# Weighing expert outputs on ScalarE, more plain scatters, and sums loaded lane by lane in a decoder layer's experts

## The reference

```python
scores = softmax(layernorm(x) @ classifier_weight.T)
_, topk_idx = top_k(scores + bias, 6)
w_full = zeros.at[token, topk_idx].add(2.5 * scores at topk_idx)
out0 = xn * w_full[:, 32:].sum(-1)                  # pass-through experts
for e in range(32):                                 # routed experts
    gate, up = split(xn @ Wgu[e].T, 2)
    out += w_full[:, e] * (silu(gate) * up @ Wd[e].T)
x = x + out
```

## Time and profile before

| what | value |
|---|---|
| median of three runs | 1355.96 us |
| the profiled execution's own time | 1358.42 us |
| its span, first to last instruction | 1356.6 us |
| mean granted TensorE clock | 0.975 |
| PE busy / DVE busy / ACT busy / POOL busy | 1219.4 / 736.0 / 872.1 / 742.6 us |
| first and last gate of the 128 tiles (L2337) | 1084.1 and 1312.2 us |
| last scatter begins (L2052) | 1326.4 us |

### The profile page before, as it was taken

One profiled execution on the slowest core, in us unless ns is written; L12 is line 12 of the kernel. 1 busy time (PEld: TensorE's weight loads), 2 busy tenths in 40 slices (PEclk: granted clock), 3 DMA queues, 4 the chain that ended last, 5 costly groups with the idle time before them and its releaser, 6 DMA issues.

```text
span 1356.6 us, 27882 instructions
## 1 busy us (share of the span) xinstructions
PE 1219.4 (90%) x8682; PEld 736.5 (54%) x8682; DVE 736.0 (54%) x2398; ACT 872.1 (64%) x1693; POOL 742.6 (55%) x814
## 2 busy tenths in 40 slices
PE   6999999999999886899999999999999799997862
PEld 4666776776676465433243324333232688986650
DVE  6666466557545648463136213623652666658863
ACT  5666456546546425678967996799989277765530
POOL 1776567557657503356026703652477577776771
PEclk9999999999999897999999999999999999999996
DMA  7976477668635521000011001010383766689988
GB/s 241 350 246 221 174 237 267 237 213 276 219 133 198 183 63 42 26 26 17 9 40 34 23 3 48 3 34 1 116 292 120 280 191 196 211 235 234 271 161 263
DMA packets 165940, 208.04 MB, mean 153 GB/s; under 512 B 13184, under 2 KB 147344, under 8 KB 165152
## 3 DMA queue, kind: packets, MB, share of 16 engines
q1 hardware_dynamic: 149664, 175.95, 39.7%
q0 software_dynamic: 16128, 30.26, 8.6%
HBM read 77.30 MB, written 128.86 MB: 152 GB/s over the span
## 4 chain that ended last, share of the span: by engine, by line
PE 56%; ACT 13%; DVE 10%; issue 9%; DMA 6%; POOL 3%; SPq 1%; ACTq 1%; DVEq 0%; POOLq 0%
PE sa_pf L354 11%; ACT xa_probs L1398 8%; PE xa_banks L1237 7%; PE xa_banks L1252 6%; PE sa_po L429 5%; PE sa_ps L403 5%; PE xa_banks L1120 5%; PE sa_ptr L414 5%; PE sa_pf L387 4%; PE mo_banks L2136 3%; DMA mo_xs<-rows 3%; DMA mo_w_all<-in_down_p 1%; PE mo_banks L2145 1%; PE mo_banks L2124 1%; ACT xa_q_aug L1344 1%
## 5 line engine op out<-in xcount | busy, mean ns | idle before, releaser
L1398 ACT ACTIVATE xa_probs<-xa_banks 128x1024 f32<-128x1024 f32 (+1 forms) x416 | 401.9, 1045 | 82.7 <-PE xa_banks L1237 81.8
L341 POOL TENSOR_SCALAR sa_probs<-sa_probs,sa_recip 128x128 f32<-128x128 f32 (+3 forms) x256 | 275.4, 1089 | 176.0 <-DVE sa_recip L592 175.8
L472 ACT ACTIVATE sa_probs<-sa_probs,sa_neg_max 128x128 f32<-128x128 f32 (+3 forms) x256 | 141.9, 555 | 148.2 <-DVE sa_neg_max L529 148.1
L1252 PE MATMUL xa_banks<-xa_probs,xa_v_one 128*17 128x512 f32 (+1 forms) x1664 | 218.7, 598 | 6.9 <-ACT xa_q_aug L1344 4.6
L1237 PE MATMUL xa_banks<-xa_q_aug,xa_k_aug 32*128 32x512 f32 (+1 forms) x1664 | 153.3, 442 | 13.4 <-issue 3.3
L2136 PE MATMUL mo_banks<-mo_xs_t,mo_gu 128*128 128x128 f32 x1024 | 138.0, 278 | 4.4 <-DVE mo_hidden_t L2337 4.4
L529 DVE CUSTOM_DVE_ANT_0 sa_probs<-sa_ps,sa_toeplitz 128x128 f32<-128x128 f32 (+3 forms) x256 | 115.5, 488 | 38.6 <-PE sa_ps L403 35.7
L2136 PEld LDWEIGHTS mo_banks<-mo_xs_t,mo_gu 128*128 128x128 f32 x1024 | 126.5, 194 | 6.6 <-ACT mo_xs_t L2186 3.5
L2193 ACT ACTIVATE mo_gu<-mo_w_all 128x512 f32 x128 | 80.7, 630 | 64.1 <-issue 49.8
L1237 PEld LDWEIGHTS xa_banks<-xa_q_aug,xa_k_aug 32*128 32x128 f32 (+1 forms) x1664 | 61.6, 179 | 106.4 <-ACT xa_probs L1398 75.7
L589 DVE COPY sa_pt<-sa_ptr 128x128 f32<-128x128 f32 (+3 forms) x128 | 62.8, 490 | 104.0 <-PE sa_ptr L414 103.9
(11 more groups left out here) (332 smaller groups left out, 2340.8 us busy)
## 6 DMA issues: line engine op xcount, KB each, us to landing
rows<-sa_blank SPq DMA_DIRECT2D x128, 548.0 KB, 3.6
mo_xs<-rows SPq DMA_DIRECT2D x128, 137.0 KB
slots<-sa_blank SPq DMA_DIRECT2D x48, 256.0 KB, 4.0
mo_slot_part<-slots SPq DMA_DIRECT2D x24, 512.0 KB, 6.1
parts<-sa_blank SPq DMA_DIRECT2D x51, 128.0 KB, 4.2
xa_raw<-in_ctx_t SPq DMA_DIRECT2D x24, 256.0 KB, 2.8
mo_w_all<-parts SPq DMA_DIRECT2D x24, 256.0 KB, 6.2
mo_w_all<-in_gate_up_p SPq DMA_DIRECT2D x2, 2816.0 KB
```

The source lines that it names most:

```text
L341: pool.tensor_scalar(probs[:, t % SLOTS, 0:w], probs[:, t % SLOTS, 0:w], recip[:, col:col + 1], None, ALU.mult).then_inc(probs_ready, 1)
L472: act.activation(probs[:, t % SLOTS, 0:w], probs[:, t % SLOTS, 0:w], ACT.Exp, bias=neg_max[:, i:i + 1], scale=-1.0, accum_out=sums[:, i:i ...
L1252: last = pe.matmul(banks[32 * i:32 * i + XD + 1, 6 + group % 2, :], v_one[b % 2][0:m, c, 4 * g + i, :], probs[0:m, (2 * j + i // 2) % RING ...
L1398: act.activation(probs[0:m, n % RING, :, :], banks[0:m, 2 * (n % 3):2 * (n % 3) + 2, :], ACT.Exp).then_inc(probs_ready, 1)
```

## The change

- `weigh` moves from DVE to ACT: in step t ACT weighs tile t-3, between `copy_rows` of t+2 and silu of t; the last three tiles follow the loop. It waits there also for `own_ready`.
- `PLAIN` goes from 72 to 80: 80 plain scatters, 48 with an add.
- The slot loads begin at tile 92 and come every 7/5 tiles, so they end at tile 124 instead of 125. Tokens are loaded at SP's tiles 48, 56 and 64.
- In the tail SP no longer waits for all lanes: when tile 125 has landed it loads its lane in four loads of 512 KB, after tile 126 that one's, and after tile 127 the last lane in eight loads of 256 KB, each of these behind the landing of one earlier load that has the same semaphore. DVE adds the first two lanes by batch (8 adds of 128x1024) and the last by chunk (8 adds of 128x512); PE's part is gone. SP stores eight chunks instead of four batches.

```diff
-PLAIN = 72
+PLAIN = 80
...
-    TOKENS_AT = {56: 0, 72: 1, 88: 2}
+    TOKENS_AT = {48: 0, 56: 1, 64: 2}
...
-    SLOT_LOAD_AT = [SLOTS_FROM + 9 * n // 5 for n in range(len(SLOT_LOADS))]
+    SLOT_LOAD_AT = [SLOTS_FROM + 7 * n // 5 for n in range(len(SLOT_LOADS))]
     SLOT_ADD_AT = [t - 2 for t in SLOT_LOAD_AT]
-    SUMS_PE = [1, 4]
-    SUM_ORDER = [0, 2, 1, 3, 5, 4, 6, 7]
+    LAST_TILES = range(N_TILES - LANES, N_TILES)
+    SLOT_LOADS_EACH = len(SLOT_LOADS) // SLOT_RING
...
         def part(c, lane, n=1):
-            at = (c * LANES + lane) * CHUNK * D
+            at = lane * TILES * D + c * CHUNK * D
...
+        def batch_landed(eng, n, b):
+            eng.wait_ge(parts_in[n * B + b], 16 * (1 + (SLOT_LOADS_EACH if n == 0 else 0)))
+
+        def chunk_landed(eng, c):
+            eng.wait_ge(parts_in[c], 16 * (2 + (SLOT_LOADS_EACH if c < B else 0)))
...
-            for i in range(SCATTERS):
-                sp.wait_ge(y_sent[i], 16 * (N_TILES // SCATTERS))
+            sp.wait_ge(gu_ready, N_TILES)
+            for n, t in enumerate(LAST_TILES):
+                lane = t % LANES
+                tile_landed(sp, t)
+                if n < LANES - 1:
+                    for b in range(B):
+                        sp.dma_start(part(2 * b, lane, 2), lane_rows(lane)[:, TT * b * D:TT * (b + 1) * D]
+                                     ).then_inc(parts_in[n * B + b], 16)
+                else:
+                    for c in range(TILES // CHUNK):
+                        batch_landed(sp, c // B, c % B)
+                        sp.dma_start(part(c, lane), lane_rows(lane)[:, c * CHUNK * D:(c + 1) * CHUNK * D]
+                                     ).then_inc(parts_in[c], 16)
...
+            def weigh(t):
+                act.wait_ge(y_psum, t + 1)
+                act.wait_ge(own_ready, t + 1)
+                if t >= Y_RING:
+                    tile_landed(act, t - Y_RING)
+                act.activation(y[t % Y_RING][:], banks[:, 4 + t % 2, 0:D], ACT.Copy, scale=own[:, t, 0:1]
+                               ).then_inc(y_ready, 1)
+
             for t in range(N_TILES):
                 if t + AHEAD < N_TILES:
                     copy_weights(t + AHEAD)
                     copy_rows(t + AHEAD)
+                if t >= 3:
+                    weigh(t - 3)
                 act.wait_ge(gu_psum, t + 1)
...
-                if t >= 2:
-                    weigh(t - 2)
...
+            for n, t in enumerate(LAST_TILES[:-1]):
+                for b in range(B):
+                    batch_landed(dve, n, b)
+                    last = dve.tensor_tensor(batch_tokens(b), batch_tokens(b), part(2 * b, t % LANES, 2), ALU.add)
+                chain.then_wait(last)
+            for c in range(TILES // CHUNK):
+                chunk_landed(dve, c)
+                dve.tensor_tensor(tokens(c), tokens(c), part(c, LAST_TILES[-1] % LANES), ALU.add
+                                  ).then_inc(out_ready, 1)
```

More of the change, by code:

```diff
@@ L1886, in experts @@
         out_ready = sem("out_ready")
-        sum_psum = sem("sum_psum")
         out_done = sem("out_done")
@@ L1896, in part, with batch_tokens @@
         def part(c, lane, n=1):
-            at = (c * LANES + lane) * CHUNK * D
+            at = lane * TILES * D + c * CHUNK * D
             return w_all[:, at:at + n * CHUNK * D]
+        def batch_tokens(b):
+            return (own_x[:] if b == LAST else acc[:, TT * b:TT * (b + 1), :]).rearrange("p t d -> p (t d)")
         def load_weights(sp, lo, hi):
@@ L1906, in first_weights @@
             load_weights(sp, FIRST_WEIGHTS // 2, FIRST_WEIGHTS)
-        def parts_landed(eng, c):
-            eng.wait_ge(parts_in[c], 16 * (LANES + len(SLOT_LOADS[c::SLOT_RING] if c < SLOT_RING else ())))
+        def batch_landed(eng, n, b):
+            eng.wait_ge(parts_in[n * B + b], 16 * (1 + (SLOT_LOADS_EACH if n == 0 else 0)))
+        def chunk_landed(eng, c):
+            eng.wait_ge(parts_in[c], 16 * (2 + (SLOT_LOADS_EACH if c < B else 0)))
         slot_rows = slots[SLOT_ROWS:, :].rearrange("(k p t) d -> p k (t d)", k=TOP_K, p=P)
@@ L1950, in run_sync @@
                 sp.dma_start(xs[:, t % X_RING, :], rows[bass.ds(at, P), :]).then_inc(xs_in[t % X_RING], 16)
-            for i in range(SCATTERS):
-                sp.wait_ge(y_sent[i], 16 * (N_TILES // SCATTERS))
-            for c in range(TILES // CHUNK):
[L1954 to L1962, removed]
+            sp.wait_ge(gu_ready, N_TILES)
[11 more added lines that the diff above has]
+                                     ).then_inc(parts_in[c], 16)
+            out_v = out.rearrange("b (t p) d -> p (b t) d", p=P)
+            for c in range(TILES // CHUNK):
+                sp.wait_ge(out_ready, c + 1)
+                sp.dma_start(out_v[:, CHUNK * c:CHUNK * (c + 1), :],
+                             tokens(c).rearrange("p (t d) -> p t d", d=D)).then_inc(out_done, 16)
+            sp.wait_ge(out_done, 16 * TILES // CHUNK)
         def more_consts(pool):
@@ L2160, in run_tensor @@
                     back(t - 2, chosen[t - 2])
[L2162 to L2169, removed]
         def run_scalar(act):
@@ L2208, in run_scalar @@
                 act.activation(silu[t % 2][:], banks[:, 2 + t % 2, 0:P], ACT.Silu).then_inc(silu_ready, 1)
+            for t in range(N_TILES - 3, N_TILES):
+                weigh(t)
         def run_vector(dve):
@@ L2338, in gate @@
                                   ).then_inc(h_ready, 1)
[L2340 to L2345, removed]
             def add_slots(n):
@@ L2364, in run_vector @@
                         add_slots(n)
-            weigh(N_TILES - 2)
-            weigh(N_TILES - 1)
             chain.then_wait(dve.tensor_reduce(zero_w[:], weights[:, :, E_ROUTED:], AX.X, ALU.add))
```

## The result

The kernel after takes 1350.1 us, the median of 13 runs (1344.97 to 1353.39), beside 1356.47 for the kernel before, measured with it. The measured ratio is 0.9946, interval 0.9934 to 0.9957; the two medians alone would give 0.9953. So it is 6 to 7 us faster. Measured again later (after_again), it came to 0.994 [0.9921, 0.996]. The forecast of 1344.3 was 0.9914 of the 1355.96 it started from: the sign and the range held, the gain is about 0.6 of what was forecast.

The account below looks back on a forecast made before the run. PE paces tiles to 80, DMA the slot-load stretch, POOL's scatters the end. Last scatter -8.0 and tail -3.7 make -11.7 us: 1358.42 profiled to 1346.7, median 2.46 lower, 1344.3 us; range 1334 to 1355.

Parts of the forecast that it names:

- Weighing on ACT, 0 before tile 80: First 80 tiles: weighing takes 0.46 us, holds ACT 0.36; 1.46 us a tile stays under PE's 1.575, so no cost.
- the 0.09 us for the operand: ACT's weighing: 0.09 us added to a plain copy's 0.369 for the per-partition scale, giving 0.46.
- rival 1: ACT becomes the bound before tile 80: 1.80 us a tile, 18 us more, 1362 us, slower; chance 0.13.
- Tokens earlier, tile 80 and tile 83: DVE's 6.29 us token wait goes; tile 80 scattered at 1216.9, tile 83 at 1222.5, some 8 us gained there.
- POOL, able to do 2.19 us a scatter, is right behind y: tile 115 at 1296: Slot-load stretch: DMA sets 2.30 us a tile, scatters keep up with y; 12 left at 1294.
- 0.9 us for later y's: ACT's weighing waits for row copies of tile t+3, so each y comes 0.9 us later, between nothing and 1.575.
- the last scatter 8.0 us earlier: End of the loop: the last adding scatter begins at 1318.4, 8.0 us earlier; bounds 2.5 and 21.6 us.
- The tail, -3.7: Tail: bytes set its length; first lane's loads start two scatters earlier, saving 3.7 us; bounds 0 and 6.
- Rival 2: POOL stays seven tiles behind, waiting for landings; it gains 2.5 us and the tail 2: 1351.5 us; chance 0.22.
- its two signs: Rival 2's signs: POOL waits for landings over 10 us, with more than 15 scatters left after the last slot load.
- Rival 3: DVE, not DMA, sets 2.06 us; freed of weighing, the loop runs ahead, POOL at 1.87: 1331 us; chance 0.10.

Follow-up runs that it names:

- a_dve: The kernel after with the weighing back on VectorE, two tiles back; ratio to before 0.992 [0.99, 0.9939].
- c_dve4: The kernel after with the weighing back on VectorE, two tiles back, and four lanes of adding scatters in place of three; ratio to before 0.9936.
- a_half: The kernel after with each slot load cut to one of its two choices, leaving half the slots' values out of the sums; ratio to before 0.9863.
- c_lanes4: The kernel after with four arrays for adding scatters instead of three, so a scatter waits for the tile four before it; ratio to before 0.9927.
- b_act: The kernel before with only the weighing moved to ScalarE, three tiles back; ratio to before 0.9984.
- the run that was to tell it: The kernel after with the weighing on VectorE, three tiles back instead of two; ratio to before 1.0038.

## Why the prediction was right in sign and too large

- **Weighing on ACT, 0 before tile 80: right, with more room than I took.** It takes 0.467 us (0.46 forecast; that is partly luck, since the exponential that gave the 0.09 us for the operand also accumulates a sum). ACT's shortest whole tile is 1088.54 to 1089.85, 1.31 us (1.46 forecast):

```profile
1088.54 0.63 ACT L2196 ACTIVATE mo_gu<-mo_w_all 128x512 f32 x1 [0.18 <-issue]
1089.07 0.36 ACT L2189 ACTIVATE mo_xs_t<-mo_banks 128x256 f32<-128x256 f32 x1
1089.34 0.47 ACT L2209 ACTIVATE mo_y<-mo_banks,mo_own 128x256 f32<-128x256 f32 x1
1089.69 0.28 ACT L2221 ACTIVATE mo_silu<-mo_banks 128x128 f32<-128x128 f32 x1
1089.85 0.64 ACT L2196 ACTIVATE mo_gu<-mo_w_all 128x512 f32 x1
```

  Issue stands ahead of the first weight copy and is missing ahead of the second, as in the earlier trace rows. So rival 1 did not come about. The first 80 gates took 0.8 and 3.0 us longer than before; but the two kernels like after with the weighing two tiles back on VectorE (a_dve, c_dve4) took 126.7 and 126.8 us, and those with it whole on ScalarE 125.0 to 128.6, so no share of ACT in it is shown. The rule of the Trainium skill that spoke for rival 1 ("ScalarE: Activation LUTs", Rules for kernel authors: multiply on VectorE) came out otherwise in the arrangement of before, where the move gained 2.2 us. In that of after it may be right (0.992 against 0.9946, not settled), but not by ACT's time. Its figure gave 0.49 us for the weighing; the trace has 0.467.
- **Tokens earlier, tile 80 and tile 83: right in the profiled execution.** Tile 80 went at 1216.3 (1216.9 forecast), tile 83 at 1222.0 (1222.5), the first slot load at 1219.5 (1220.5); after_again is 2.4 us later in all three.
- **"POOL, able to do 2.19 us a scatter, is right behind y: tile 115 at 1296": the step that failed.** The prices were right: 23 x 1.42 + 33 x 0.58 + 30 x 0.82 = 76.4 us of work in 70, 1.09, and the share was 1.08 (1.05 in after_again). But I divided them as if each tile's row load, scatter and slot loads went in step, so that gate and scatter would both come every 2.30 us. They don't: the gates, behind SP's row loads, came every 2.12 us and the scatters every 2.43, and POOL fell nine tiles behind instead of running right behind y. What sets a scatter's pace is the time to the landing of the one three before it, which grew from 6.95 to 7.28 us where POOL waited for it, and is 6.46 in a_half (five waits); a sum of DMA work does not hold that term. Nor was 1.05 full, as four lanes show (1.11). Half the slots' bytes (a_half) or one lane more (c_lanes4) each brought the last scatter 8 to 9 us nearer to gate 80 (10 against after_again), so the landings behind the slot loads are shown as the cause. The Trainium skill ("DMA: Bandwidth & Descriptors", SWDGE vs HWDGE vs iDMA) says that an engine takes turns between its internal queues, fed by SP's loads and by POOL's scatters; no run shows the turns themselves. The software queue's share is no fixed one: 35.9% in after, 41.1% with four lanes, 45.6% with half the slots' bytes.
- **0.9 us for later y's: about right.** From tile 60 to 79 the weighing starts 4.02 us after the gate, 3.39 before, so 0.6 more. From tile 87 to 119 it is 5.38 (before 4.38, a_dve 4.67), 1.0 us more; there it stands behind row copies that wait for the DMA, as shown under a_dve. I had named the queue and not what it waits for there.
- **Stretch by stretch:** I forecast the last scatter 8.0 us earlier, all of it behind gate 80. From gate 80 on it is 5.7 and 4.4 us earlier in the two executions, and the first 80 gates take 0.8 and 3.0 us of that back.
- **The tail, -3.7: right.** It is -3.8 and -3.0. DMA is busy all through it (a share of 1.05 at 381 GB/s), so the bytes set it as said. SP's issues:

```profile
1320.82 4.77 SPq L1962 DMA_DIRECT2D mo_w_all<-parts  x8
1329.57 6.59 SPq L1967 DMA_DIRECT2D mo_w_all<-parts  x8
1337.83 4.16 SPq L1972 DMA_DIRECT2D out<-mo_acc  x6
1342.03 1.46 SPq L1972 DMA_DIRECT2D out<-xa_x  x2
```

- **The rivals.** Rival 2 had the loop right: its two signs, more than 10 us of waits for landings and more than 15 scatters left, are there with 15.7 and 17, and its 1351.5 is nearer to 1350.1 than the forecast (as ratios 0.9967 and 0.9914, beside 0.9946). But these signs told little, since before itself had 13.5 us and 15 scatters left. It had 0.22 and deserved more, since 2.19 against 2.30 was its own argument. Rival 3 was right in its first half: freed of the weighing, the loop ran ahead (b_act, 36 gates for 34), but POOL did not follow.
- **The parts and the whole.** Tail, tokens and ScalarE each alone give 0.31, 0.2 and 0.16%, together 0.67, beside the 0.54 of the whole that has the plain scatters and denser slot loads besides. With some 0.12 to either side of each, that is no clear difference; it does not show a gain from the plain scatters and the denser loads either. In the arrangement of before, the weighing on ScalarE gains 2.2 us; in that of after, taking it away seems to gain some 3.5 (0.9946 against 0.992), which the intervals do not settle.

What stays open is whether those 3.5 us are there, and how much of them are late y's and how much a loop that runs ahead and crowds the scatters; the run that was to tell it slowed the loop instead. The waits of after_again speak for the second.

## What to carry to other kernels

Where several streams share a busy DMA, don't divide the total evenly. A stream whose transfers wait for their own landings goes at the time to a landing divided by how many may be under way, so price that time beside its bytes; one more under way can be worth as much as halving the other stream's bytes. Work put on an engine's queue behind an operation that waits for a transfer inherits that wait, so a price per instruction is only half its cost. A relieved engine is worth something only if the stream that ends last gets what it frees.

## What was not expected

The loop's start moves: in the 14 profiles of this study the first gate begins between 1080.0 and 1085.7 us, though ahead of it only the two kernels with four lanes differ (they clear a fourth array), so a single profile can't tell 3 us at its end, and the stretches above are counted from a gate. A scatter's pace depends on what it must wait for more than on the DMA share: 35 scatters went in 68 us at a share of 1.11 with four lanes, 29 at 1.08 with three.
